# Storing the expert tiles' result rows: GpSimd's indirect store in place of SyncE's whole-tile store

## What is computed

```python
def _moe_forward(x, gate_w, w_gate_up, w_down, shared_w_gate_up, shared_w_down):
    ...
    shared_out = jax.nn.silu(g_s) * u_s @ shared_w_down.T
    ...
    topk_vals, topk_idx = jax.lax.top_k(probs, TOP_K)          # TOP_K = 2 of 16 experts
    topk_vals = topk_vals / jnp.sum(topk_vals, axis=-1, keepdims=True)
    ...
    act = jax.nn.silu(g) * u
    out_e = jnp.einsum('eti,ehi->eth', act, w_down)
    moe_out = jnp.einsum('eth,te->th', out_e, combine)
    return (moe_out + shared_out).reshape(orig_shape)
```

## Time and profile before

| | |
|---|---|
| median of 3 runs | 2028.82 us (2020.81 to 2033.82) |
| the profiled execution | 2021.97 us, its span 2020.1 us |
| mean granted TensorE clock | 0.993 of full speed |
| run 0, tile loop | about 1668 to 1765 us |
| run 1, tile loop | about 1885 to 1982 us |

### The profile page before, as it was taken

How to read it: one execution, slowest core, us unless ns; L and a number is a source line. 1 busy time by engine, 2 the same in 40 slices (tenths; PEclk the granted TensorE clock), 3 DMA queues, 4 the chain that set the end, 5 groups by cost and what they waited for, 6 DMA issues and landing times.

```text
span 2020.1 us, 38785 instructions
## 1 busy us (share of the span) xinstructions
PE 1966.5 (97%) x11776; PEld 1634.7 (81%) x11776; DVE 1504.9 (74%) x2838; ACT 1181.0 (58%) x2570; POOL 1034.4 (51%) x907
## 2 busy tenths in 40 slices
PE   5999999999999999999999999999999989998998
PEld 4888888888888888888888888888888868876887
DVE  7998599859976997699679967985899572176315
ACT  4785388538843874497449645963696335432442
POOL 1497059616941793279228823981497025250433
PEclk8999999999999999999999999999999999999999
DMA  2552145214512351334134313530352049931896
GB/s 101 160 169 56 49 120 168 57 45 121 162 47 74 111 147 43 92 113 127 43 92 135 111 38 97 150 101 28 107 162 83 21 138 379 340 114 42 310 378 199
DMA packets 143910, 253.95 MB, mean 126 GB/s; under 512 B 21448, under 2 KB 37832, under 8 KB 143696
## 3 DMA queue, kind: packets, MB, share of 16 engines
q1 hardware_dynamic: 134848, 231.35, 36.7%
q0 software_dynamic: 7520, 16.80, 2.7%
q10 hardware_dynamic: 1328, 3.15, 0.4%
HBM read 233.38 MB, written 25.69 MB: 128 GB/s over the span
## 4 chain that ended last, share of the span: by engine, by line
PE 90%; DVE 6%; ACT 1%; issue 1%; POOL 0%; DMA 0%; DVEq 0%; ACTq 0%; SPq 0%
PE bank L1627 60%; PE bank L1739 7%; PE bank L1930 6%; PE bank L1753 5%; PE bank L1693 4%; PE bank L1942 3%; PE bank L1721 2%; PE bank L1917 1%; DVE Y L1230 1%; DVE spare L1318 1%; PE bank L1712 1%; PE bank L1760 1%; PE bank L1635 1%; DVE Y L1239 1%; POOL wl L743 0%
## 5 line engine op out<-in xcount | busy, mean ns | idle before, releaser
L1627 PE MATMUL bank<-xh,wh 128*128 128x512 f32 x1288 | 523.4, 406 | 10.7 <-POOL wl L713 4.0
L1627 PE MATMUL bank<-xh,wl 128*128 128x512 f32 x1288 | 504.4, 392 | 0.0
L1627 PE MATMUL bank<-xl,wh 128*128 128x512 f32 x1288 | 502.2, 390 | 0.0
L713 POOL TENSOR_TENSOR wl<-raw,wh 128x512 fp32r<-128x512 f32 x144 | 192.8, 1344 | 460.8 <-ACT wh L861 460.8
L1230 DVE SCALAR_TENSOR_TENSOR Y<-bank,cpar,Y 128x511 f32<-128x511 f32 (+2 forms) x384 | 286.8, 747 | 24.4 <-ACT Y L905 15.4
L1627 PEld LDWEIGHTS bank<-xh,wh 128*128 128x128 f32 x1288 | 242.9, 189 | 60.6 <-POOL wl L713 4.9
L1627 PEld LDWEIGHTS bank<-xh,wl 128*128 128x128 f32 x1288 | 242.0, 188 | 54.2
L1627 PEld LDWEIGHTS bank<-xl,wh 128*128 128x128 f32 x1288 | 243.2, 189 | 45.5 <-issue 0.5
L730 POOL TENSOR_TENSOR Y<-Y,gt 128x512 f32<-128x512 f32 x128 | 184.9, 1444 | 94.5 <-DVE gt L1284 92.8
L1292 DVE TENSOR_TENSOR al<-Y,ah 128x512 fp32r<-128x512 f32 x128 | 95.6, 747 | 169.1 <-ACT ah L963 169.1
L1627 PE MATMUL bank<-wh,ah 128*128 128x512 f32 x544 | 213.7, 393 | 2.8 <-DVE X L1539 2.2
(11 more groups left out here) (232 smaller groups left out, 4072.0 us busy)
## 6 DMA issues: line engine op xcount, KB each, us to landing
mem<-c_rows SPq DMA_DIRECT2D x128, 256.0 KB, 3.8
mem<-wffn_d SPq DMA_DIRECT2D x62, 512.0 KB
E<-e_rows SPq DMA_DIRECT2D x256, 96.0 KB, 3.4
raw<-wconv_d SPq DMA_DIRECT2D x80, 256.0 KB, 3.0
cv<-c_rows SPq DMA_DIRECT2D x64, 256.0 KB, 3.9
spare<-c_rows SPq DMA_DIRECT2D x64, 256.0 KB, 4.2
raw<-wgate_d SPq DMA_DIRECT2D x64, 256.0 KB, 2.7
raw<-wout_d SPq DMA_DIRECT2D x64, 256.0 KB, 2.6
```

The source lines that it names most:

```text
L713: inc(pool.tensor_tensor(wl[:, W_SLOT[p], :], raw[:, R_SLOT[p], :], wh[:, W_SLOT[p], :], ALU.subtract), w_lo)
L1627: got = mm(out, l, r, start=first and n == 0, stop=last and n == 2)
```

## The change

`tile_out` is gone from SyncE. GpSimd has `t_scatter`, which stores tile `tau-7` (`BEHIND`) behind gather `tau`, and the last seven behind the loop. It is an indirect DMA to `slots_y`: VectorE makes a table `slot_to` of each slot's own number, plus an amount that puts it out of bounds where the slot is empty, and rows out of bounds are left out. A second table, `slot_own`, is made once at the start. Since the empty slots are no longer written, `slots_y` is filled once with rows of the input: four DMAs from DRAM to DRAM, issued by GpSimd in ticks 28, 30, 32 and 34 of group 0.

```diff
@@ sync
-            def tile_out(run, tau):
-                sp.wait_ge(ty_ok, job(run, tau) + 1)
-                sp.dma_start(slots_y[tau * P:(tau + 1) * P, :], ybuf[tau % Y_RING]).then_inc(
-                    ty_out[tau % Y_RING], 16)
...
-                    if k:
-                        tile_out(run, k - 1)
@@ gpsimd
+            step(pool.iota(iota_i[:, :], pattern=[[P, 32]], base=0, channel_multiplier=1))
+            step(pool.tensor_copy(slot_own[:, :], iota_i[:, :]))
...
+            def fill(n):
+                rows = slice(n * TOK, min((n + 1) * TOK, TILES * P))
+                pool.dma_start(slots_y[rows, :], x_d[0:rows.stop - rows.start, :]).then_inc(slots_filled, 16)
+
             def tick(i, k):
+                if opening(i) and k in FILL_AT:
+                    fill(FILL_AT.index(k))
...
+            def t_scatter(run, tau):
+                if tau == 0:
+                    pool.wait_ge(toks_ok, 2 * run + 2)
+                    pool.wait_ge(slots_filled, 16 * len(FILL_AT))
+                pool.wait_ge(ty_ok, job(run, tau) + 1)
+                pool.indirect_dma_start(slots_y, bass.IndirectOffsetOnAxis(ap=slot_to[:, tau:tau + 1], axis=0),
+                                        ybuf[tau % Y_RING], None, bounds_check=TILES * P - 1,
+                                        oob_is_err=False).then_inc(ty_out[tau % Y_RING], 16)
...
                 for tau in range(TILES):
                     t_gather(run, tau)
+                    if tau >= BEHIND:
+                        t_scatter(run, tau - BEHIND)
...
+                for tau in range(TILES - BEHIND, TILES):
+                    t_scatter(run, tau)
@@ vector, toks_out
-                    step(TS(empty[:, :], found, 0.0, float(2 * TOK), ALU.is_equal, ALU.mult))
+                    step(TS(empty[:, :], found, 0.0, float(2 * TILES * P), ALU.is_equal, ALU.mult))
                     STT(toks[:, :], found, -1.0, empty[:, :], ALU.add, ALU.add).then_inc(toks_ok, 1)
+                    TTn(slot_to[:, :], slot_own[:, :], empty[:, :], ALU.add).then_inc(toks_ok, 1)
```

More of the change, by code:

```diff
@@ L27 @@
 GU_RING, DN_RING, X_RING, Y_RING, H_RING = 4, 3, 4, 4, 3
+BEHIND = 7
+FILL_AT = (28, 30, 32, 34)
 LOG1P = (1.0, -0.49999905, 0.33330005, -0.24954559, 0.19678117, -0.15311863, 0.10614265, -0.057064202,
@@ L136, in hybrid_layer @@
         empty = sb("empty", [P, 32])
+        slot_own = sb("slot_own", [P, 32])
+        slot_to = sb("slot_to", [P, 32], u32)
         own_f = sb("own_f", [1, 32])
@@ L292, in hybrid_layer @@
         lane_ok, xn_out = sem("lane_ok"), sem("xn_out")
+        slots_filled = sem("slots_filled")
         tw_in = [sem(f"tw_in{q}") for q in range(GU_RING)]
@@ L361, in hybrid_layer, with opening @@
         BANKS = EARLY + LATER[len(EARLY):]
+        def opening(i):
+            return isinstance(i, int) and i == 0
         def big_bank(i, k):
@@ L762, in _ @@
                 pool.wait_ge(own_ok, run + 1)
-                pool.wait_ge(toks_ok, run + 1)
+                pool.wait_ge(toks_ok, 2 * run + 1)
                 pool.wait_ge(xn_out, 32 * (run + 1))
```

## The result

The changed kernel takes 2046.35 us in the median of 5 runs (2045.42 to 2047.23), the kernel before, measured beside it, 2026.71 us in the median of 5 (2020.81 to 2033.82). The ratio is 1.0098, with a 95% interval of 1.0081 to 1.0114: slower by about 1%, some 20 us. The profiled execution has a span of 2044.7 us against 2020.1. The forecast was 2030, an addition of 1.4 us; the time lies inside its range (2019 to 2047), but at the upper end of it and at the boundary between "within 1%" and "slower". The two traces differ by 24.6 us, more than the medians do, because the execution of the kernel before that was traced is 4.7 us faster than its median.

The account below looks back on a forecast made before the run. The prediction took TensorE to bound the loop. Terms 0 + 1.0 + 0.1 + 0.3 + 0 = +1.4 us, added to 2028.82 (the profiled 2021.97 plus 6.85 to the median), gave 2030, range 2019 to 2047.

Parts of the forecast that it names:

- GpSimd becomes the bound, mildly: Tile loops: rival with 1.49 us per indirect store, GpSimd late, 2043, up to 2047; chance 0.16.
- the fills: Group 0 ticks: four DRAM to DRAM copies, each 5.3 us, just hidden ahead of output-weight loads; 0.
- TensorE bounds the loop, so removing the stores is worth 0: Tile loops: TensorE never waits for a DMA, so SyncE's issue time and 3.9 MB fewer a run give 0.
- fewer bytes make it steadier: Tile loops: rival that a tenth less traffic brings executions down to the fastest, -8, 2021; chance 0.06.
- s = 1.00 for an indirect store, 2.60 of 3.08 us per tile: Tile loops: GpSimd's store issue taken from the gather's median; gather, store and gaps leave 0.48 us per tile.
- the two rivals in which GpSimd becomes the bound: Tile loops: mild, 2043 to 2047, chance 0.16; plain, over 1% from 1.64 us per store, 2066 at 2.0, chance 0.13.
- TensorE waits 1.0 us in run 0 for a gather near tile 22, 0 in run 1: Tile loops: gather 22 of run 0 is 7.1 us late with room of 6.1; +1.0 us.
- the landing L: Tile loops: time for a gather's data to land, taken as 4.0 us, between 2.63 and 6.3.
- ScalarE's side has the same room: Tile loops: stores have 5.9 us of room before ScalarE reuses a buffer; not counted twice; a ScalarE wait would show error.
- D = 1.4 to 2.1, covered by a slack of 2.05: End of each run: fetches start 1.4 to 2.1 us later, last lands by 2010.70, needed at 2012.75; 0 to 0.1 us.
- the rival by name: Group 0 ticks: the fills hold the weights up, +4.6 us if half as fast; chance 0.03.
- Tables 0.3: Slot tables: one more VectorE instruction for `slot_to` per run, 2 x 0.15 = 0.3 us; `slot_own` 0.

Follow-up runs that it names:

- e8: Changed kernel without fills, first run's stores writing all rows, with GpSimd's product of 3.65 us cut into four parts: 2025.52 us, 1.0020 of the kernel before.
- e9: The kernel before, unchanged, traced again beside the changed kernel on one chip: 2023.21 us (one run).
- e10: The changed kernel, unchanged, run again beside the kernel before on one chip: 2038.86 us, 1.0090.
- e11: The changed kernel with its fills cut into rows of 2 KB, beside the unchanged changed kernel: 2026.38 us, 1.0025.
- e6: No fills, SyncE storing whole tiles as in the kernel before, plus three short GpSimd multiplications per tile in place of an indirect store: 2035.65 us, 1.0072.
- e12: As e8, with the last seven tiles of each run stored whole by SyncE: 2022.36 us, 1.0004 of the kernel before.
- e2: Changed kernel without fills; the first run's indirect stores write all rows, the second's leave empty slots out: 2038.92 us, 1.0047 of the kernel before.
- e4: Changed kernel without fills, indirect stores writing all 128 rows of every tile in both runs: 2040.58 us, 1.0047 of the kernel before.
- group 1: The experiments that shared one chip: e1, e2, e3 and e4; the kernel before took 2030.44 us there.
- e3: No fills, SyncE storing whole tiles as in the kernel before, plus a GpSimd indirect store per tile that writes nothing: 2039.76 us, 1.0045.
- e1: The kernel before with only the four fills added on GpSimd's queue, SyncE still storing whole tiles: 2042.34 us, 1.0057.
- e7: Changed kernel without fills, GpSimd storing whole tiles with plain DMAs: 2026.88 us, 1.0025 of the kernel before.
- group 3: The runs that shared one chip: e9, e10, e11 and e12; the kernel before took 2021.64 us there.

## Why the prediction came out as it did

The number holds by luck. The forecast was +1.4 us and the change cost 17 to 20; it stays inside the range only because the range reached up to 2047 for a rival, "GpSimd becomes the bound, mildly", that didn't come. Most of the time went to a term that the sum had at nothing, the fills.

*TensorE bounds the loop, so removing the stores is worth 0.* Right. e8 has the stores off SyncE in both runs, and in run 1 the bytes of the empty rows off the DMA engines too; its loops (97.0 and 95.6) are those of e9 (97.4 and 96.9), and so is loop 1 of e10 and e11 (95.7 and 96.1). The rival "fewer bytes make it steadier" didn't come either: the changed kernel's executions beside the result lie within 1.8 us, but none is below 2045, and e11 has 2023.2 to 2028.8 where the kernel before has 2017.9 to 2024.8.

*s = 1.00 for an indirect store, 2.60 of 3.08 us per tile.* Right: 1.015 us, 0.30 between two. The bounds 0.43 and 1.49 weren't reached; the two rivals in which GpSimd becomes the bound didn't come, and e6 shows what they would have looked like.

*TensorE waits 1.0 us in run 0 for a gather near tile 22, 0 in run 1.* The mechanism is right, on the chip without bursts to the tile: 1.7 us at tile 21, and 0.7 behind the product. The term was sized at 1.0 and measured 2.4. The mis-sized part is the landing L. In e9, where no gather is late, they land 4.4/5.9/7.3 us (shortest, median, longest) from the start of the issue, so the median L is 4.9 and not 4.0. The gather of tile 21 is issued until 1740.95 and its rows are taken up at 1746.45: L = 5.5, a room of 4.6. It starts 6.5 us late (the transposes of tile 17 end at 1732.65), near the forecast 7.1, and 6.5 - 4.6 = 1.9 against the measured 1.73.

*ScalarE's side has the same room.* Right in size: ScalarE waits 0.9 us once for a store (e10), and no wait of TensorE follows from it. By the prediction's own words such a wait was a sign of being wrong, and it is one of L again: the stores land 2.1/5.0/7.4 us from the start of their issue.

*The end: D = 1.4 to 2.1, covered by a slack of 2.05.* D was right (1.74; in e10 4.95 - 3.00 = 1.95), the slack was the error. It took the landing of the second fetch, 2.63 us, for that of the last one, which has 15 others ahead of it: "lands by 2010.70" is the step that failed. In the kernel before, all that the rows show is a landing within 2012.75 - 2008.07 = 4.68 us; in e10 it took 5.50 (2029.48 - 2023.98). Whatever slack there was is smaller than that, and the end cost 3.2 to 3.7 us instead of 0.1. In the trace of the result a second late piece stands beside it, TensorE's 2.4 us for VectorE (L1552), which e10 hasn't.

*The fills: 0, "a whole fill ahead costs 5.3, just hidden", or 4.6 at half the rate.* This is the step that failed most: 12 to 14.5 us. The forecast had the rival by name, but priced it as the wait for one fill's bytes, and gave it 3 in 100. Two things were wrong. The loads met fills that themselves landed after 8.9 to 12.7 us, not 5.3. And it reasoned that an engine which takes its queues in turn lets a small load pass. A load of 256 KB is 128 rows of 2 KB, some 8 for each of 16 DMA engines. If a row may have to stand behind one piece of 64 KB, then taking turns is what makes it slow. e11 shows that the size of the pieces is the cause, and e10's packets show the turns: a round of pieces takes some 3 us, and behind three of the rounds only 14 to 16 of the loads' 512 rows pass, about one for each engine. The load issued at 182.4 meets seven rounds, of which six begin behind its issue, and lands after 22.5 us. Why more rows pass in some gaps than in others is open. The Trainium skill, "DMA: Bandwidth & Descriptors", section "Queues, rings and completion order", says that the turn changes between packets of several descriptors; the forecast cited it and read it as a promise that small loads pass, and with descriptors of 64 KB it is the reverse. The trace agrees that turns are taken, and not with that reading (7.6 us against 22.5).

*Tables 0.3.* Below what can be seen: loop 0 begins 0.4 and 1.1 us later in e12 and e11 than in e9, and 0.2 earlier in e8 than in the trace of before.

*Not in the forecast: the bursts of the increments.* In the trace of the result and in those of e2 to e4 the loops lost some 6 and 3 us or more that no wait for gathers or stores explains. The trace that the forecast was made from has such pauses too, 23 and 26, and its loops are no longer for them (95.4 and 95.9, against 97.4 and 96.9 in e9). But that is one of the fastest executions: on the chip of group 1 the kernel before has a median of 2030.44 against 2022.12 and 2021.64 on the other two, and no trace shows where those 8 us go. That the second stream of GpSimd's DMAs makes them cost time is shown by e3 against e1 (103.3 and 101.3 us against 96.7 and 96.8, SyncE's stores in both, one trace each). Why increments are held, and why on some chips only, is open. It wasn't tried whether plain DMAs of GpSimd do it as well, since e7 ran on a chip without bursts.

Together, on the chip of group 3 (e10 less e9, span): +13.0 by the fills with the tables, +0.7 in loop 0, -0.9 between, -1.2 in loop 1, +3.7 at the end, 15.4 us. In the pair of the result it is 24.6, and 9.5 us of that are in the loops. By the medians the two measurements lie closer together: 19.6 us and 17.2.

## What to carry to other kernels

A DMA that is "off the path" has a shape as well as a size: one whose source and destination are both contiguous is cut into long pieces, and a small load that meets it can wait for one piece per row. Move such a copy to where no load with a deadline is in flight, or break its contiguity. And when a slack is computed from a landing time, take it from the same place in the queue: in e10 the last of 16 gathers lands 5.5 us behind its issue, the second 2.6.

## What the runs showed of the hardware

- An indirect store of 128 rows takes GpSimd 1.02 us whether all of them (e4: 1.019), 66 on average (the changed kernel: 1.015) or none (e3: 1.017) are in bounds.
- A plain store of the same 128 rows takes GpSimd 0.578 us, two indirect DMAs have 0.30 us between them.
- The changed kernel's loops are 3.5 us longer in the trace of the result than in e10 (101.6 and 99.2 against 98.1 and 95.7), and the traces differ in whether semaphore increments come evenly or in bursts some 0.65 us apart. With bursts an increment can stand 5.0 (changed) or 6.3 us (e3) behind the end of its matmuls, without them it stands within 0.02.
- While a DRAM to DRAM copy in pieces of 64 KB is under way, one piece takes a median 2.94 us, 16 at a time, and another queue's rows of 2 KB go in between the pieces, at times one per piece (e10).
- In the pause of TensorE for the late load the granted clock falls to the lower level, and it stays there for 10.2 us (e1, e10) to 13.7 us (the changed kernel), part of them after the matmuls have begun again. That is in what a late load costs.
